# A graph layer's count stage: node features turned by DMA instead of TensorE, and the attention products grouped by weight half

## The reference, cut to what matters

```python
h = jnp.maximum(_layernorm(x, axis=-1), 0.0)
HW = h @ W
s = HW @ a[:OUT_F, 0]
t = HW @ a[OUT_F:, 0]
e = leaky_relu(s[row] + t[col], negative_slope=0.2)
ex = jnp.exp(e - segment_max(e, row)[row])
att = ex / segment_sum(ex, row)[row]
agg = segment_sum(att[:, None] * h[col], row)
out = silu(agg) @ base_w.T + einsum('nip,oip->no', b_splines(agg), spline_w)
...
x = x + out
h = jnp.maximum(_layernorm(x, axis=-1), 0.0)
...
x = x + three graph convolutions of h
```

## Time and profile before

| | us |
|---|---|
| median of 3 runs | 613.38 |
| lowest, highest of them | 612.81, 620.52 |
| the profiled execution, own time | 613.95 |
| its span | 611.8 |
| mean granted clock of TensorE in it, as a share | 0.982 |
| PE busy, DVE busy, ACT busy, GpSimd busy | 578.0, 435.9, 332.7, 42.9 |

### The profile page before, as it was taken

How to read it: one execution, slowest core, us unless ns; L and a number is a source line. 1 busy time by engine, 2 the same in 40 slices (tenths; PEclk the granted TensorE clock), 3 DMA queues, 4 the chain that set the end, 5 groups by cost and what they waited for, 6 DMA issues and landing times.

```text
span 611.8 us, 9451 instructions
## 1 busy us (share of the span) xinstructions
PE 578.0 (94%) x3797; PEld 379.8 (62%) x3797; DVE 435.9 (71%) x717; ACT 332.7 (54%) x420; POOL 42.9 (7%) x40
## 2 busy tenths in 40 slices
PE   4998949999989999999999999999999999999994
PEld 2766848889645555555555555687557855587552
DVE  7999699997679999993499779362474335542555
ACT  4568466569999989891898234044132333142112
POOL 1056100000000000000000030042000020000000
PEclk9999779999998999999999999999999999999998
DMA  9960078662600000000000001240200000000112
GB/s 306 356 239 2 3 180 186 142 90 50 237 1 0 2 2 0 1 1 0 1 2 1 1 1 43 91 193 0 70 1 0 1 1 2 1 0 1 41 43 84
DMA packets 40459, 36.36 MB, mean 59 GB/s; under 512 B 28414, under 2 KB 30078, under 8 KB 40288
## 3 DMA queue, kind: packets, MB, share of 16 engines
q1 hardware_dynamic: 40416, 35.76, 19.5%
HBM read 23.36 MB, written 5.84 MB: 48 GB/s over the span
## 4 chain that ended last, share of the span: by engine, by line
PE 80%; DVE 13%; ACT 2%; issue 2%; DMA 1%; DVEq 1%; ACTq 0%
PE bank L1689 36%; PE bank L1774 21%; PE bank L1731 13%; PE bank L1647 2%; DVE MSK L1140 2%; DVE EX L1153 2%; PE bank L1569 2%; DVE HL L1169 2%; DVE EX L1157 1%; PE bank L1652 1%; DVE OR L1013 1%; DVE BHL L1239 1%; PE bank L1558 1%; PE bank L1524 1%; DMA AT<-HL 1%
## 5 line engine op out<-in xcount | busy, mean ns | idle before, releaser
L1689 PE MATMUL bank<-BHL,WKh 128*128 128x418 f16 x1152 | 206.4, 341 | 2.1 <-DVE BHL L1239 2.1
L1689 PEld LDWEIGHTS bank<-BHL,WKh 128*128 128x128 f16 x1152 | 111.7, 97 | 96.2 <-DVE BHL L1239 2.5
L1774 PE MATMUL bank<-C,YH 128*128 128x418 f16 x360 | 122.4, 340 | 0.0
L1774 PE MATMUL bank<-C,YL 128*128 128x418 f16 x360 | 122.3, 340 | 0.0
L1470 DVE SCALAR_TENSOR_TENSOR Z<-bank,yback,dvb 128x418 f32<-128x418 f32 x36 | 23.4, 651 | 52.1 <-PE bank L1774 52.1
L950 ACT ACTIVATE bnc<-bnm,tiny 128x1 f32<-128x1 f32 x12 | 3.5, 296 | 91.7 <-DVE bnm L1478 91.7
L1774 PEld LDWEIGHTS bank<-C,YH 128*128 128x128 f16 x360 | 35.3, 98 | 28.8 <-issue 0.8
L1647 PE MATMUL bank<-AT,hH 128*128 128x256 f16 (+1 forms) x200 | 45.8, 277 | 7.7 <-DMA AT<-HL 7.7
L1774 PEld LDWEIGHTS bank<-C,YL 128*128 128x128 f16 x360 | 35.2, 98 | 28.0
L912 ACT ACTIVATE YH<-bank,dvl 128x512 f16<-128x512 f32 x30 | 20.4, 686 | 56.6 <-PE bank L1731 56.6
L1416 DVE SCALAR_TENSOR_TENSOR YL<-bank,dvl,YH 128x512 f16<-128x512 f32 x30 | 22.0, 749 | 39.1 <-ACT YH L912 39.1
(11 more groups left out here) (220 smaller groups left out, 963.7 us busy)
## 6 DMA issues: line engine op xcount, KB each, us to landing
WKf<-in_wk SPq DMA_DIRECT2D x9, 1024.0 KB, 6.6
c_scratch<-C SPq DMA_DIRECT2D x10, 320.0 KB, 3.0
C<-c_scratch SPq DMA_DIRECT2D x1, 3200.0 KB, 10.3
GWf<-in_gwT SPq DMA_DIRECT2D x3, 1024.0 KB, 11.5
XT<-in_xT SPq DMA_DIRECT2D x1, 2500.0 KB, 9.3
outT<-Z SPq DMA_DIRECT2D x3, 625.0 KB, 3.0
hx<-in_x SPq DMA_DIRECT2D x1, 1280.0 KB, 6.9
Wt<-in_WT SPq DMA_DIRECT2D x1, 1024.0 KB, 9.1
```

Source lines behind the costliest of these rows:

```text
L1689: ins = mm(bank[:, 4 * (g % 2) + o, 0:G], lhs, rhs, start=(u == 0 and q == 0 and i == 0), stop=(u == UNITS - 1 and q == PAIR - 1 and i == 2))
L1774: ins = mm(bank[:, u % YB, 0:G], Y[:, j, o * P:(o + 1) * P], C16[:, j, g * G:(g + 1) * G], start=(j == 0 and i == 0), stop=(j == NT - 1 an ...
```

## The change

Four things, all ahead of the spline network.

- Each tile of h is split in halves right behind its relu: ACT rounds it (`rounded`, `hH`), DVE computes `hL` (`low_half`), GpSimd has no part in it. Both halves go through a DMA transpose on the SP queue into `hT`, now f16 and large enough for all tiles. The 20 transposes stand behind the loads of `wk` and `gpar` in that queue. PE's f32 transposes and ACT's copies of `hT` and `strow` are gone.
- The products with W a are f16, with W a scaled to a unit and split in halves too (`wsplit`, a chain of small DVE operations in `bounds`). They come in three sets, tiles 0 to 3, 4 to 7 and 8 to 9: `rows` in groups 11, 16 and 18 makes the broadcast row with 12 products each, `cols` in groups 12, 17 and 18 makes the columns.
- In a pair of tiles PE does `attend_high` of all four banks, then `attend_low` of all four.
- `C16` is stored one tile later, behind the transposes of tiles 1 to 5 instead of 0 to 4.

The bound on the exponent's argument is replaced by a fixed `SHIFT` in units of the vector's length, which adds three small operations on DVE behind the first `largest` (`source_columns`) and a scale to the exponential.

```diff
-TURN_AT = (5, 6, 8, 9, 11, 12, 14, 15, 16, 17)
+H_AT = (5, 6, 7, 8, 9, 11, 12, 13, 14, 15)
+ROWS_IN = (11, 16, 18)
+COLS_IN = (12, 17, 18)
+H_SETS = ((0, 4), (4, 8), (8, 10))
-ROWS_AT = (11, 17)
+ROWS_AT = (13, 18)
...
+            sp.wait_ge(wa_done, 1)
+            for b, (t0, t1) in enumerate(H_SETS):
+                for t in range(t0, t1):
+                    sp.wait_ge(h_high, t + 1)
+                    sp.dma_start(hT[:, 0, :, t * P:(t + 1) * P], hH[:, t, :], transpose=True).then_inc(hT_in[b], 16)
+                    sp.wait_ge(h_low, t + 1)
+                    sp.dma_start(hT[:, 1, :, t * P:(t + 1) * P], hL[:, t, :], transpose=True).then_inc(hT_in[b], 16)
...
-                for t in range(2 * s, min(2 * s + 2, NT)):
+                for t in range(2 * s - 2, 2 * s) if 1 <= s <= NT // 2 else ():
                     sp.dma_start(c16_dram[:, t, :], C16[:, t, :]).then_inc(c16_out, 16)
...
-            for t in range(NT):
-                pool.wait_ge(h_high, t + 1)
-                nc.gpsimd.tensor_tensor(hL[:, t, :], hx[:, t, :], hH[:, t, :], ALU.subtract).then_inc(h_low, 1)
...
+            def rounded(t):
+                act.wait_ge(h_rows, t + 1)
+                nc.scalar.copy(hH[:, t, :], hx[:, t, :]).then_inc(h_high, 1)
...
+                    if n == H_AT[t]:
                         activations(t)
+                        rounded(t)
...
-            def rounded(t):
-                dve.wait_ge(h_rows, t + 1)
-                V.tensor_copy(hH[:, t, :], hx[:, t, :]).then_inc(h_high, 1)
+            def low_half(t):
+                dve.wait_ge(h_high, t + 1)
+                V.tensor_tensor(hL[:, t, :], hx[:, t, :], hH[:, t, :], ALU.subtract).then_inc(h_low, 1)
...
+                    if n == H_AT[t] + 1:
+                        low_half(t)
...
+            def source_columns():
+                dve.wait_ge(st_set, 1)
+                V.tensor_tensor(sbend[:, :], st[:, :, 0:1].rearrange("p t k -> p (t k)"),
+                                st[:, :, 1:2].rearrange("p t k -> p (t k)"), ALU.add)
+                dve.drain()
+                V.tensor_scalar(sbend[:, :], sbend[:, :], BEND, None, ALU.mult)
+                dve.drain()
+                V.tensor_scalar(near[:, :], sbend[:, :], SHIFT, bnd[:, 2:3], ALU.subtract, ALU.mult).then_inc(sbend_set, 1)
...
+            def rows(b):
+                t0, t1 = H_SETS[b]
+                pe.wait_ge(hT_in[b], 32 * (t1 - t0))
+                pe.wait_ge(wn_set, 1)
                 for c in range(DC):
+                    for i, k in ((0, 0), (1, 0), (0, 1)):
+                        ins = mm(trow[:, t0 * P:t1 * P], down(wsplit[:, i, c, 1:2]), hT[:, k, c, t0 * P:t1 * P],
+                                 start=(c == 0 and i + k == 0), stop=(c == DC - 1 and k == 1))
+                ins.then_inc(rows_in, 1)
+
+            def cols(b):
+                for t in range(*H_SETS[b]):
+                    for c in range(DC):
+                        for k in range(2):
+                            ins = mm(bank[:, 2, ST_AT + 2 * t:ST_AT + 2 * t + 2], hT[:, k, c, t * P:(t + 1) * P],
+                                     wsplit[:, 0:2 + k:1 + k, c, 0], start=(c == 0 and k == 0),
+                                     stop=(c == DC - 1 and k == 1))
+                ins.then_inc(cols_in, 1)
...
+                for b in range(len(H_SETS)):
+                    if n == ROWS_IN[b]:
+                        pe.wait_ge(ctl_set, 1)
+                        rows(b)
+                    if n == COLS_IN[b]:
+                        cols(b)
...
                 for k in range(DC):
                     if i >= 1:
                         pe.wait_ge(agg_out, DC * (i - 1) + k + 1)
-                    attend(i, k)
+                    attend_high(i, k)
+                for k in range(DC):
+                    attend_low(i, k)
```

More of the change, by code:

```diff
@@ L215, in build @@
         lnr = small("lnr", [2, NT])
-        st = small("st", [NT, COLS])
+        st = small("st", [NT, 2])
+        sbend = small("sbend", [NT])
         mx = small("mx", [3, NT])
         wss = small("wss", [1])
-        bnd = small("bnd", [2])
+        bnd = small("bnd", [5])
         near = small("near", [NT])
@@ L314, in build @@
         bound_set = sem("bound_set")
-        h_turned = sem("h_turned")
-        h_cols = sem("h_cols")
-        strow_done = sem("strow_done")
-        strow_set = sem("strow_set")
-        st_done = sem("st_done")
+        hT_in = [sem(f"hT_in{b}") for b in range(len(H_SETS))]
+        wn_set = sem("wn_set")
+        rows_in = sem("rows_in")
+        cols_in = sem("cols_in")
+        sbend_set = sem("sbend_set")
         st_set = sem("st_set")
@@ L628, in statistics @@
                     act.wait_ge(x_in, 32)
-                nc.scalar.activation(JST[:, 0, :], hx[:, t, :], ACT.Identity, accum_out=mv[:, 0, t:t + 1])
+                nc.scalar.activation(JST[:, :], hx[:, t, :], ACT.Identity, accum_out=mv[:, 0, t:t + 1])
                 act.drain()
@@ L668, in vectors @@
                 both = bank[:, 2, WA_AT:WA_AT + 2 * DC].rearrange("p (c k) -> p c k", k=2)
-                nc.scalar.copy(wcol[:, :, 0:2], both)
-                nc.scalar.mul(wcol[:, :, 2:3], both[:, :, 0:1], BEND)
-                nc.scalar.mul(wcol[:, :, 3:4], both[:, :, 0:1], -BEND).then_inc(wa_set, 1)
-                act.wait_ge(wa_set, 1)
-                nc.scalar.activation(wjunk[:, :], wcol[:, :, 1:2].rearrange("p c k -> p (c k)"), ACT.Square,
-                                     accum_out=wsum[:, 0:1]).then_inc(wa_squared, 1)
+                nc.scalar.copy(wraw[:, :, :], both).then_inc(wa_set, 1)
+                nc.scalar.activation(wjunk[:, :, :].rearrange("p c k -> p (c k)"), bank[:, 2, WA_AT:WA_AT + 2 * DC],
+                                     ACT.Square, accum_out=wsum[:, 0:1]).then_inc(wa_squared, 1)
             def vector_bound():
@@ L970, in _ @@
             V.memset(later[0:1, :], 0.0)
-            for k, v in enumerate([1.5 - j for j in range(TWINS)] + [-2.0, 2.0, 1.0]):
+            for k, v in enumerate([1.5 - j for j in range(TWINS)] + [-2.0, 2.0, 1.0, SHIFT]):
                 V.memset(cen[:, k:k + 1], v)
@@ L1550, in vector_norm @@
                 mm(bank[:, 2, NORM_AT:NORM_AT + 1], ones[:, :], wsum[:, 0:1], start=True, stop=True).then_inc(wa_norm, 1)
-            def turn(t):
-                pe.wait_ge(h_rows, t + 1)
-                pe.wait_ge(consts_set, 2)
-                if t >= 1:
-                    pe.wait_ge(h_cols, t)
-                for c in range(DC):
-                    ins = nc.tensor.transpose(bank[:, 3, c * P:(c + 1) * P], hx[:, t, c * P:(c + 1) * P], ident[:, :])
-                ins.then_inc(h_turned, 1)
@@ L1637, in _, with attend_high @@
                 block_squares(i)
-            def attend(i, k):
+            def attend_high(i, k):
                 out = sums_of(i, k)
-                t0, t1 = GROUP_TILES[i]
-                for s in range(t0, t1):
+                for s in range(*GROUP_TILES[i]):
                     q, full = place(s)
@@ L1647, in attend, with attend_low @@
                         mm(out, lhs[:, j, k * P:(k + 1) * P], columns_of(i, 0, j), start=(j == 0 and lhs is hH), stop=False)
-                for s in range(t0, t1):
+            def attend_low(i, k):
+                out = sums_of(i, k)
+                for s in range(*GROUP_TILES[i]):
                     q, full = place(s)
```

123 lines of the change are left out of this document (45 added, 78 removed).

## The result

| | before | after |
|---|---|---|
| median, us | 613.84 (4 runs) | 626.09 (4 runs) |
| lowest, highest, us | 612.81, 620.52 | 624.66, 628.07 |
| profiled execution, its span, us | 613.95, 611.8 | 627.28, 625.5 |
| T, the first masked maximum, us | 66.98 | 78.02 |
| first long product of the spline, us | 155.98 | 171.19 |

A forecast was written before the change was run, and what follows sets the result against it. It took DVE, then mostly PE's f32 dot products, to hold the count stage up to T, and T to move the end. 613.95 + 7.1 (later T) + 0.9 (attention stage) = 622.0 us, range 614 to 627.

The forecast's parts named there:

- The new wait: Count stage, group 11: PE ready for `rows(0)` at 45.4 waits 3.1 us for the first transposes, landing at 48.5.
- on the line between them 0.51 + 0.4 x 0.86 = 0.85, which I take: SP queue: issue of a 512-wide transpose put at 0.85 us, between a plain 0.5 and the wide 1.37.
- rival 3: SP queue: a transpose's issue costs 1.37 us whatever its width; T 76.5 to 78.6, time 624.4 to 626.5; chance 0.14.
- The clock: Count stage: PE at its lower clock, 4.7 us each for `rows(0)` and `rows(1)`; `rows(2)` 1.3 at the upper level.
- the relief of 8.7 us: Count stage, DVE: without GpSimd's halves, nine long `OM` shorten from 1.44 to 0.47 us, 8.7 us in all.
- even if all rows cost nothing: Bound in the count stage: with `rows` free, DVE's list ends T at 64.9, 2.1 us earlier than before.
- rival 4: Count stage: DVE's relief decides, PE's sets never hold the list; T 64.9, time 612.8 or 611.5; chance 0.05.
- Attention stage: From T to the spline: the change costs 0.7 + 0.2 = 0.9 us, between 0 and 2.
- PE ends the stage where it did, within 1 us: Attention stage: despite grouped products and waits for banks of 0.4 to 1.4 us, PE's end moves less than 1 us.
- the gap of 2.08 at 183.71 swallows that: Spline: PE's 2.08 us gap, for a DVE product, absorbs PE's shift of within 1 us from the attention stage.
- rival 5: Whole change: it doesn't do what it says, PE not relieved or GpSimd still busy; no size; chance 1 in 50.
- rival 2: First transposes bound by their issue, not their data: landing at 46.7, 1.8 us sooner, time 620.2; chance 0.15.

The follow-up runs named there:

- filler: Kernel after, with 15 unused 128x512 f16 products in PE's wait for the first set of transposes; 624.21 us, 1.015 of before.
- low on DVE: Kernel before, with the low halves of h subtracted by DVE instead of GpSimd, PE's f32 dot products kept; 616.32 us, 1.004 of before.
- by bank: Kernel after, with each bank in the attention stage again getting its high and then its low products; 625.52 us, 1.020 of before.
- pair transposes: Kernel after, with one 128 x 1024 transpose for two tiles of a half, ten instructions for twenty; 622.31 us, 1.016 of before.
- rows late: Kernel after, with `rows` in groups 16, 18, 19 and `cols` in 17, 19, 19, ACT's copies in 17 and 19; 621.51 us, 1.015 of before.
- loads later: Kernel after, with the last two of nine `wk` loads issued behind the first set of transposes; 622.27 us, 1.014 of before.
- scale operand: Kernel before, with the ten exponentials' scale a column of ones in SBUF instead of the number 1; 614.61 us, 1.002 of before.
- bias operands: Kernel before, with -1 and -LEAK of the bias columns from SBUF and `near` computed behind the first masked maximum; 613.45 us, 1.000 of before.
- rows spread: Kernel after, with one transpose for two tiles, `rows` products spread over groups mostly in threes, high and low products bank by bank; 615.47 us, 1.007 of before.
- spread and folded: As rows spread, with ACT's second copy of the rows one group earlier and one `source_columns` operation folded into the weights; 615.44 us, 1.004 of before.
- the filler in the kernel before: Kernel before, with 16 unused 128x512 bf16 products on PE behind the counts of groups 3 and 4; 622.89 us, 1.013 of before.

## Why the prediction was right, and where its sizes were off

I had forecast 622.0 us, range 614 to 627; the median is 626.09. Direction, places and order of the mechanisms held, two terms were too small: T moved by 11.04 us for my 7.1, and the rest of the program by 2.7 (4.17 less 1.5) for my 0.9.

- **The new wait.** It is where I put it, at `rows(0)` in group 11, with the counts, ACT's relu and rounding and `low_half(6)` behind it. I had 3.1 us; it is 5.84. The step is "on the line between them 0.51 + 0.4 x 0.86 = 0.85, which I take". I had transposes at 1.3 to 1.4 us and a plain DMA at 0.5, and interpolated by width. But all transposes of that trace are 128 x 1280 (the two forms are the high and the low half), and the plain DMA is another kind of instruction, so nothing in it showed an effect of width. It is 1.26 for 512 columns and 1.31 to 1.33 for 1024. That is rival 3, to which I gave 0.14. Its upper bound, T at 78.6 and 626.5 us, is within 0.6 us of what came (78.02 and 626.09), and that is in part luck. It had the set issued at 48.3 and landed 2.7 us later; the queue in fact got to the first transpose at 38.77 instead of 37.3 and took 2.65 us over it, so the set was issued at 50.63, and it landed only 1.37 us later. It also had 0.9 us for the attention stage and the spline, where 2.7 came, and more of `rows` at the lower clock than there was.
- **The clock.** I took 4.7 us for the first two sets, and the upper level for the third. Measured 5.28, 4.45 and 1.47 in the timeline, 11.2 for my 10.7; filler shows that the first would take 2.76 at the upper level. Right in kind, 0.5 off in sum. The two long sets took from 3.9 to 5.3 us in the runs that keep them in one piece behind a wait, so 0.5 is within what the clock does from run to run.
- **DVE.** `OM` at 0.48, the relief of 8.7 us, is there. A subtraction is 0.69, not 0.6. The bound "even if all rows cost nothing" was an answer to a question that the list never asks; with everything spread T is 68.45, so rival 4 would have needed more than a landing in time. The run "low on DVE" says the same from the other side.
- **ACT.** A rounding takes 0.63 us where I had 0.5, and this piece stands in the chain three times from 39 us on.
- **Attention stage.** I priced it at 0.9 us between 0 and 2, and it is 4.17, of which the rest gives back 1.5, because a clock that fell in the attention stage didn't fall at the spline's gap. The 4.17 are 1.77 (by bank), 0.7 (grouping) and 1.7 (clock). Three steps failed. I looked at `source_columns` (0.7, right) and not at the operands: numbers that became columns in SBUF make the bias operations 0.06 us longer each and the exponential 0.09, together some 1.6 of the 2.2 us that it takes longer from the first to the last masked maximum (65.5 for 63.3); the three small operations are the rest. "PE ends the stage where it did, within 1 us" was right for the grouping itself (0.7). But I had not asked what a wait of 2.5 us does to PE's clock: 1.7 us. And "the gap of 2.08 at 183.71 swallows that" is wrong in every trace: the gap ends 27.7 to 27.9 us behind the first long product wherever that is, for DVE's list waits for PE's last sums (`agg_unit`) before it makes the inputs that PE then waits for. What the stage loses is lost.
- **GpSimd, PE's f32 work** (rival 5): gone, as the lists showed.
- **Transposes and their rate.** In the stretch below the queue only issues transposes (DMA share, GB/s are the last two):

```profile
52.00:56.00 4.00, 4.00 (x10) 1.43 (x11) 0.00 (x0) 0.00 (x0) 0.00 (x0) 1.00 0.50 102
```

102 GB/s at a share of 0.50 is some 204 GB/s for a full share, as against 332 at 0.97 for the loads. The Trainium skill, "Advanced Engine Details and Errata", section X-Bar Transpose (TRN2), has a transposing DMA as fast as a plain one; this trace has it at 0.6 of that. It made no difference: back to back transposes fill half of the DMA engines, so the issue bounds them at either rate, which is what the page's rule would have led to (rival 2) with the right price for an issue. The 204 is an estimate, and the comparison is rough: the loads come from HBM and the transposes stay in SBUF, and the share is no strict fraction (it reads 1.48 from 42 to 45 us of this trace). But the 128 x 1024 transposes of pair transposes moved 192 GB/s at a share of 1.01, from 49.64 to 50.97.

## What to carry to other kernels

Before work moves to a DMA queue, count its instructions and price each by the nearest row of the same kind, whatever the size: one size of one kind gives no slope, and a row of another kind doesn't supply it. Before a wait goes into the list of an engine that others feed on, ask what stands behind it; the same products made T 11 us later as whole sets with a wait in the middle of the list, and 1.5 us in pieces of three with half as many transposes. And when an immediate number becomes a column, read each operation that takes it: 60 and 90 ns an operation, in a loop of ten tiles, were more than the three operations that I had counted.

## What the runs showed of the hardware that I had not expected

- The SP queue takes 1.26 us to issue a DMA transpose of 128 x 512 and 1.31 to 1.33 for 128 x 1024, within SBUF, f16. While 1 MB loads were in flight, one took 5.56 us.
- The profile's granted clock doesn't always tell the level at which products run. From 52 to 56 us in the row above it is 1.00, while twelve 512-wide products take 5.28 us, 0.44 each; in rows late it is 0.50 for the same pace, and filler has 2.76 us for twelve. The duration of the products decides.
- Behind gaps of 2.1 to 2.5 us on PE the products took 1.5 to 1.7 us more in all, at a granted clock of 0.57 to 0.66 over the next 4 to 5 us, in forty products of 128 x 256 or in the first long products of the spline. Not each such gap does so: loads later shows none behind its wait in the attention stage, and scale operand, bias operands, rows spread, spread and folded and the filler in the kernel before show none at the spline's gap. What decides that stays open.
- The f32 work of the count stage ran at either level in executions with the same instructions, T between 65.6 and 73.0. The f16 form in its spread placement scatters less: 615.2 to 617.3 in ten runs, as against 611.1 to 621.9 in nineteen of before, of which fifteen stay below 619.6.
- A scale operand from SBUF instead of a number made a 128 x 1280 exponential 0.09 us longer, a scalar operand a 128 x 1 operation of DVE 0.06.
